# A score pair moved ahead of a tile, and the PSUM pairs of a round dealt out anew, in a recurrent attention and feed-forward kernel

## The reference, cut to what matters

```python
scores = jnp.einsum('bhqd,bhkd->bhqk', Qr, Kr) * DH ** (-0.5)
causal = jnp.triu(jnp.ones((t, t), dtype=bool), 1)
scores = jnp.where(causal, jnp.finfo(scores.dtype).min, scores)
pattern = jax.nn.softmax(scores, axis=-1)
heads = jnp.einsum('bhqk,bhkd->bqhd', pattern, Vh).reshape(b, t, d)
...
x = x + s * g
```

## Time and profile before

| | |
|---|---|
| time, median of 3 runs | 890.26 us (889.07 to 891.26) |
| the profiled execution's own time | 892.28 us |
| its span, first to last instruction | 890.5 us |
| mean granted TensorE clock | 0.967 |
| busy: TensorE, VectorE, ScalarE, GpSimd | 90%, 64%, 56%, 47% of the span |

### The profile page before, as it was taken

How to read it: one execution, slowest core, us unless ns; L and a number is a source line. 1 busy time by engine, 2 the same in 40 slices (tenths; PEclk the granted TensorE clock), 3 DMA queues, 4 the chain that set the end, 5 groups by cost and what they waited for, 6 DMA issues and landing times.

```text
span 890.5 us, 14271 instructions
## 1 busy us (share of the span) xinstructions
PE 805.7 (90%) x5136; PEld 486.3 (55%) x5136; DVE 571.8 (64%) x1016; ACT 500.3 (56%) x687; POOL 421.4 (47%) x472
## 2 busy tenths in 40 slices
PE   3867899887989999999999999999999999999976
PEld 2645777766755555555555555545555554555523
DVE  3997454324776777666676677676767666776444
ACT  3344453532355667566765666764675757666560
POOL 3776573553741455125670544543384424746311
PEclk9998899989899999999999999999999999999987
DMA  8445134525502312232344342234433232532131
GB/s 274 142 148 183 64 109 135 166 78 193 136 1 73 91 53 61 84 107 75 93 116 144 99 128 74 79 121 120 122 111 105 80 109 66 159 96 94 57 127 47
DMA packets 61294, 96.21 MB, mean 108 GB/s; under 512 B 10344, under 2 KB 27432, under 8 KB 61224
## 3 DMA queue, kind: packets, MB, share of 16 engines
q1 hardware_dynamic: 59640, 93.47, 34.4%
q10 hardware_dynamic: 1584, 1.84, 0.6%
HBM read 58.06 MB, written 36.95 MB: 107 GB/s over the span
## 4 chain that ended last, share of the span: by engine, by line
PE 56%; DVE 10%; ACT 5%; issue 2%; POOL 1%; DMA 1%; SPq 0%; ACTq 0%; DVEq 0%; POOLq 0%
PE ps L288 14%; PE ps L1281 12%; PE ps L1265 10%; PE ps L298 8%; PE ps L1242 7%; DVE ps L1515 3%; DVE mx L1520 3%; PE ps L1317 3%; ACT probs L1411 2%; PE ps L1253 1%; ACT a_sb L308 1%; DVE a_sb L329 1%; ACT x_ffn L1423 1%; DMA spread<-scr_inv 1%; DVE y_sb L335 1%
## 5 line engine op out<-in xcount | busy, mean ns | idle before, releaser
L1411 ACT ACTIVATE probs<-ps 128x1024 f32<-128x1024 f32 (+1 forms) x320 | 292.9, 940 | 109.3 <-PE ps L1265 107.8
L1520 DVE TENSOR_REDUCE mx<-ps 128x4 f32<-128x512 f32 (+1 forms) x192 | 215.5, 1133 | 103.7 <-PE ps L1242 62.1
L1137 POOL TENSOR_SCALAR_AFFINE_SELECT probs<-probs 128x256 f32<-128x256 f32 (+1 forms) x192 | 92.8, 488 | 279.9 <-ACT probs L1411 279.5
L1515 DVE CUSTOM_DVE_ANT_0 ps<-ps,tri 128x384 f32<-128x384 f32 (+1 forms) x256 | 154.2, 647 | 31.3 <-PE ps L1242 31.3
L1281 PE MATMUL ps<-probs,v_ones 128*32 128x512 f32 (+3 forms) x1536 | 157.7, 498 | 5.5 <-POOL probs L1137 4.8
L1265 PE MATMUL ps<-q_s,k_s 64*128 64x512 f32 (+3 forms) x768 | 148.8, 413 | 10.3 <-DVE mx L1515 4.6
L1265 PEld LDWEIGHTS ps<-q_s,k_s 64*128 64x128 f32 x768 | 67.1, 184 | 158.7 <-issue 80.9
L1242 PE MATMUL ps<-k_s,q_s 48*128 48x512 f32 (+3 forms) x768 | 121.7, 366 | 8.7 <-PEq L379 5.2
L288 PE MATMUL ps<-xh,wug_hi 128*128 128x512 f32 x256 | 110.6, 432 | 16.8 <-DVE a_sb L329 16.4
L343 POOL TENSOR_TENSOR a_sb<-a_sb,u_sb 128x512 f32<-128x512 f32 x64 | 82.3, 1288 | 61.5 <-ACT u_sb L316 61.5
L288 PE MATMUL ps<-xh,wug_lo 128*128 128x512 f32 x256 | 102.6, 401 | 0.0
(11 more groups left out here) (134 smaller groups left out, 1084.6 us busy)
## 6 DMA issues: line engine op xcount, KB each, us to landing
scr_qk<-kinds SPq DMA_DIRECT2D x64, 256.0 KB, 2.3
q_s<-scr_qk SPq DMA_DIRECT2D x64, 128.0 KB, 2.8
k_s<-scr_qk SPq DMA_DIRECT2D x64, 128.0 KB, 3.0
scr_heads<-o_raw SPq DMA_DIRECT2D x30, 256.0 KB, 2.1
x_sb<-in_x SPq DMA_DIRECT2D x8, 512.0 KB, 4.4
scr_v<-v_st SPq DMA_DIRECT2D x16, 256.0 KB, 2.6
q_s<-scr_qk SPq DMA_DIRECT2D x64, 64.0 KB, 2.9
k_s<-scr_qk SPq DMA_DIRECT2D x64, 64.0 KB, 3.0
```

What stands on the lines that cost most here:

```text
L1137: pool.affine_select(out=part, in_=part, compare_op=ALU.is_ge, fill=0.0, base=0, pattern=pattern, channel_multiplier=-1).then_inc(cut, 1)
L1411: act.activation(probs[:, n % 2, p, :, 0:w], ps[:, bank:bank + 2, 0:w], ACT.Exp, scale=SCALE).then_inc(exp_ok, 1)
L1515: last = dve.tensor_tensor_reduce(part_of, part_of, sh.tri[:, CH - w:CH], 1.0, LOWEST, ALU.add, ALU.max, mx[:, v % 2, kind, h, i % TPC:i % ...
L1520: last = dve.tensor_reduce(out[:, :, pairs[0]:pairs[0] + n], ps[:, banks[0]:banks[0] + 2, 0:n * w].rearrange('p e (x k) -> p e x k', x=n), ...
```

## The change

The first step's score pair 1 goes ahead of tile 0 in TensorE's order, so that both score pairs of the first step stand side by side. It writes pair B, where it wrote C. Tile 0 comes behind it and writes pair C, where it wrote B. Tiles 1, 2 and 3 keep B, C and C. The order of all else, and the lists of the other engines, stay. By the planner's rule the holders before each item change with it: score pair 1 of the first step now follows score pair 1 of the last round's second step, tile 0 follows tile 3 of the last round, tile 1 follows score pair 1 of the first step, and tile 2 follows tile 0.

```diff
     s0, s1 = ([('scores', now[0], now[1] + n, p) for p in range(2)] if now else [] for n in range(2))
     early = len(jobs) if now else len(jobs) // 2
-    for what, banks in zip(s0 + s1[:1], (PAIR_A, PAIR_C, PAIR_A)):
+    for what, banks in zip(s0 + s1[:1], (PAIR_A, PAIR_B, PAIR_A)):
         pair_of[what] = banks
-    pair_of.update(zip(tiles, (PAIR_B, PAIR_B, PAIR_C, PAIR_C) if now else (PAIR_B, PAIR_C, PAIR_B, PAIR_C)))
+    pair_of.update(zip(tiles, (PAIR_C, PAIR_B, PAIR_C, PAIR_C) if now else (PAIR_B, PAIR_C, PAIR_B, PAIR_C)))
     pair_of.update((what, PAIR_B) for what in s1[1:])
-    for what in s0[:1] + tiles[:1] + s0[1:] + s1[:1] + tiles[1:3 if now else 2]:
+    for what in s0 + tiles[:1] + s1[:1] + tiles[1:3 if now else 2]:
         give(what, pair_of[what])
...
                 if now:
                     u, s = now
                     scores(u, s, 0)
+                    scores(u, s, 1)
                 if tiles:
                     max_tile(*tiles[0])
                 if now:
-                    scores(u, s, 1)
                     if s:
                         weigh(u, s - 1)
```

## The result

The changed kernel takes 904.12 us (median, 899.12 to 905.4) against 890.76 us for the kernel before in the same session: a ratio of 1.0152, 95% interval 1.0126 to 1.0177, 13.4 us slower. The direction was the one forecast. The size is twice the forecast, and the time lies outside the range.

A forecast was written before the change was run, and what follows sets the result against it. TensorE was taken to bound the kernel, with 56% of the chain. Terms of +8.8 us in rounds, less 0.2 in the last unit and 1.4 swallowed, gave 7.2, kept as 6.7: 897.0 us for the median, range 889.5 to 903.

The forecast's parts named there:

- The order alone: Swapping score pair 1 and tile 0 on TensorE, both of one slot, leaves the values where they were: 0 us.
- The masked tile: In rounds 0 and 2 masked tile 0 stands next to the values: 0.1 us per late round, 0.3 and 0.5 us.
- late round: A round whose score pair 1 stands over 0.1 us behind its kind's closest spacing: 39 of 74, 13.6 us.
- the last unit: Score pair 1 in round 0 waits less, -0.4 us; in rounds 2 and 3 an exponential costs +0.2: -0.2.
- The exponential's wait at tile 1: Tile 1 now waits for score pair 1's exponential, formerly tile 2: rounds 3 +2.4, 0 +3.0, 2 +1.9 us.
- The wait for tile 3: Third item of a round still waits for VectorE's read of the last round's tile 3: the 13.6 us stay.
- Round 1: Tile 2, no longer tile 1, waits for tile 0's read: -0.8 us early, +1.2 late, +0.5 in three others.
- What later waits swallow: Later waits in the rounds hide part of the delay: 1.4 us off, then 7.2 cut to 6.7.
- VectorE late: Rival: VectorE idles through tile 0's matmuls and each late round pays: +13 us and beyond, 901 to 906; chance 0.09.
- Faster by the change of mode: Rival: one TensorE tiling-mode switch saved per round, -7.4 us against +6.7: 890, or 886; chance 0.03.

The follow-up runs named there:

- shortexp: Half of the exponential of score pair 1 of each first step but the very first left out: kernel before 887.13 us, changed kernel 897.94 us.
- both edits: Tile 0's masks and half of the exponential of first-step score pair 1 left out: kernel before 886.38 us, changed kernel 891.44 us.
- round_3: The change, order and pairs, in round 3 of each unit alone, against the kernel before: 892.61 us against 890.36, ratio 1.0024.
- order_alone: The new TensorE order with the old pairs, against the kernel before: 918.18 us against 889.74, ratio 1.0312.
- pairs_alone: The new pairs with the old TensorE order, against the kernel before: 915.45 us, ratio 1.0291.

## Why the prediction was right or wrong

*The order alone, "leaves the values where they were: 0".* Right where no tile is masked: the values of a round 3 start at S + 0.90 in both traces, and side by side pairs take 0.73 us.

*The masked tile: "0.1 us later in each late round of these kinds".* This is the step that failed: the term was mis-sized. It stands in the sum with 0.3 + 0.5 = 0.8 us and measured 6.0 us when nothing covers it, and 2.5 us (7.9 - 5.4) on top of the exponential's wait. I took the difference of two record lengths, 0.58 against 0.50, for a difference of slots. Records overlap; what the next item waits is the spacing of the starts, and that is 0.61 us from tile 0 to the values against 0.43, and with tile 0's later start 0.27 us in a round 0, mostly 0.06 to 0.13 in an early and 0.17 in a late round 2. And I booked it in 8 rounds only, those in which I saw nothing else wait. In the other 22 it is there as well, next to the exponential's wait. In rounds 0 it covers the same 0.25 us, which is why `shortexp` brought so little.

*What else was too low.* Without the half-clock stretch the traces grew by 14.6 us for a forecast of 6.7 with all deductions, so 7.9 us are missing. In rounds 0 and 2 they are 9.3 for 5.7: the masked tile 1.7 more, the exponential's wait 0.5 more (5.4 for 4.9), and and 1.4 that stay with both edits, half of it in the very first round. Rounds 1 have 0.8 more, rounds 3, rounds 4 and the last unit 0.5 each. The last 1.9 are what I took off for later waits, which the lengths of rounds already contain. So the masked tile is the largest of the terms but not most of the gap; the rest is small terms, all on the same side and in part unexplained. One of them I left out altogether: a tile that starts behind a wait is followed 0.1 us later. Tile 2 paid that before in rounds 3, so nothing was lost there, but in rounds 0 it is new (0.47 for 0.39 us).

*The exponential's wait at tile 1.* Right: place and time to 0.01 us in rounds 3; 2.7 us for 2.2 in all, 2.3 by the median of `round_3`, and -0.1 with the exponential shortened. In rounds 2 the wait ends at S + 2.62 as forecast.

*The wait for tile 3.* Right that it stays at the third place. `order_alone` and `pairs_alone` show what it costs at the second: 26 to 28 us, and so the prediction's 0 for the order alone holds with these pairs only.

*Round 1.* The late ones came as worked out (below, S = 430.33: tile 0, tile 1, tile 2), with tile 2 at S + 3.05, 0.36 us late where 0.22 was forecast. The read ends at 433.24 and tile 2 starts 0.14 us behind it, where I had taken 0.05. The early ones gained nothing where -0.8 us was forecast, with the same lag (read's end 547.66, tile 2's load 547.77).

```profile
431.29 0.50 PE L1242 MATMUL ps<-k_s,q_s 48*128 48x512 f32 x2 [0.29 <-DVE mx L1515]
...
432.84 0.39 PE L1242 MATMUL ps<-k_s,q_s 48*128 48x512 f32 x2
433.38 0.50 PE L1242 MATMUL ps<-k_s,q_s 48*128 48x512 f32 x2 [0.15 <-DVE mx L1515]
```

*What later waits swallow.* I took off 1.4 us and then 0.5 more by the words "of which I keep 6.7". In the traces the shifts at tile 2 add up to 16.1 us and those of the rounds' lengths to 12.7; 1.6 of the difference is the half-clock stretch, so some 1.8 were swallowed. That was right in size.

*VectorE late.* Not the main cause, although the time it would give, +13 us, is the one measured: that number came by chance. With both edits the difference fell from 13.4 to 5.1 us while VectorE's list stayed. In rounds 3 with the short exponential tile 0 still stands 0.23 to 0.48 us later than before, and the rounds grow by nothing. VectorE does set what rounds 1 pay, by its read of tile 0. Its idle time ahead of reads did grow as forecast, from 40.6 to 55.9 us ahead of reads that wait for a masked tile.

*Faster by the change of mode.* It didn't come: the values of a round 3 start at S + 0.90 in either order, so no switch between tile and score pair was saved.

Open: with both edits 5.1 us are left by the medians and 3.8 in the rounds by the traces. Of the 3.8, 1.6 lie in rounds 1, for which the wait for tile 0's read was seen but not taken away by a run. Another 1.5 lie in rounds 0, half of it in the very first, and 0.6 in rounds 4; their causes were not followed. Rounds 2 come to -0.1, with 0.7 carried into two of them. No run shortened that read: one of fewer columns would take the maximum of fewer scores. Why some items start 0.11 to 0.14 us behind the end of the read they wait for (tile 0 of a round 0 at 539.01, the read before it over at 538.87; tile 2 of rounds 1) and others 0.05 behind it is open too.

## What to carry to other kernels

When an item is moved in an in-order list, price its slot by the distance from its start to the start of what follows in the same company (behind a wait, ahead of the values), not by its record's length: the first said 0.18 us more here, the second 0.08. Where two costs fall on the same instruction, write down the time at which each would let it go: the later one is paid, the other is hidden, and taking away one of them shows next to nothing. A buffer's holder and an item's place in the order are one decision: half of this change cost 26 to 28 us, all of it 13.

## What was not expected of the hardware

A tile that starts behind a wait is followed 0.1 us later than one in a running row: tile 1 to tile 2 took 0.34 us in rounds 3 of the changed kernel and 0.23 with the short exponential; the masked tile 1 of a round 0 took 0.47 us (540.69 to 541.16) and 0.39 in the kernel with both edits (532.89 to 533.28). In these places a new wait cost its length and 0.1 us. Where an older wait went away in exchange, its 0.1 us went too: in rounds 3 the first job stood 0.37 us behind tile 2 before (519.36 to 519.73) and about 0.27 after. This was read from traces and not made an experiment of its own.
